# Weight quantisation chunks moved from the projection stage into the attention loop of an eight-core transformer layer

## What is computed

```python
xn = _layernorm(x)                                  # x: 16 x 2048 x 1024, f32
q, k, v = xn @ w_q, xn @ w_k, xn @ w_v              # 1024 -> 128, one head
s = (softmax(q @ k.T / sqrt(128)) @ v * mask) @ w_o
scale = max(abs(kernel)) / 7                        # kernel: 1024 x 1024
w = clip(round(kernel / scale), -8, 7) * scale
g = silu(xn @ w + bias + (xn @ a) @ b)
return x + s * g
```

## Time and profile before

| what | us |
|---|---|
| median of the runs (1221.0 and 1221.43) | 1221.22 |
| the profiled execution's own time | 1224.67 |
| its span on the slowest core, core 4 | 1222.8 |
| spans of the eight cores | 1209.9 to 1222.8 |
| mean granted TensorE clock of the cores | 0.909 to 0.917 |

### The profile page before, as it was taken

The page is one execution under the profiler, slowest core; times in us unless marked ns, Lnnn a source line. Parts: engine busy times, 40 slices in busy tenths (PEclk is TensorE's granted clock), DMA queues, the critical chain, the costliest instruction groups (busy, mean ns, idle before and its releaser), DMA issues.

```text
span 1222.8 us, 12399 instructions; the slowest of 8 cores (1209.9 to 1222.8 us)
## 1 busy us (share of the span) xinstructions
PE 923.5 (76%) x4453; PEld 499.5 (41%) x4453; DVE 428.5 (35%) x632; ACT 347.6 (28%) x662; POOL 21.8 (2%) x30
## 2 busy tenths in 40 slices
PE   0745363788885988888892789788885888989795
PEld 0422131466662334343431454366664333334332
DVE  2646755333323122221304665423332123132303
ACT  1322331554541211102011343445452110112110
POOL 4010000000000000000000000000000000000000
PEclk9987786899996999999997799999997989899998
DMA  5440301000001105150314320000001104123032
GB/s 142 148 139 23 121 24 45 18 1 1 1 1 69 69 1 172 35 172 35 103 35 172 127 115 1 0 2 1 1 1 69 35 35 155 53 71 136 3 135 104
DMA packets 25310, 78.54 MB, mean 64 GB/s; under 512 B 3601, under 2 KB 6673, under 8 KB 25250
## 3 DMA queue, kind: packets, MB, share of 16 engines
q1 hardware_dynamic: 18338, 52.57, 13.5%
q10 hardware_dynamic: 4608, 16.78, 3.4%
q0 software_dynamic: 2304, 8.39, 2.1%
HBM read 60.95 MB, written 16.78 MB: 64 GB/s over the span
## 4 chain that ended last, share of the span: by engine, by line
PE 59%; DVE 14%; ACT 12%; DMA 8%; issue 6%; POOL 0%; DVEq 0%; ACTq 0%; SPq 0%; POOLq 0%
PE PA L162 47%; PE PS L162 6%; PE PF L162 6%; ACT xfh L199 3%; DMA y<-xq 3%; DVE xfl L417 3%; ACT A_sb L208 3%; ACT ATf L199 3%; DVE g_sb L194 2%; DMA wstpair<-kern 2%; DVE xq L189 2%; DVE ssum L234 1%; DMA wstpair<-x 1%; DVE nm L234 1%; DMA wstpair<-wq 1%
## 5 line engine op out<-in xcount | busy, mean ns | idle before, releaser
L162 PE MATMUL PA<-xfh,q_sb 128*128 128x512 bf16 x512 | 132.0, 404 | 7.3 <-ACT g_sb L208 3.8
L162 PE MATMUL PA<-ATf,Vt 128*128 128x256 f32 x512 | 114.3, 381 | 18.2 <-ACT ATf L199 18.2
L208 ACT ACTIVATE g_sb<-PA,invsc 128x512 f32<-128x512 f32 x64 | 43.7, 687 | 279.8 <-PE PA L162 241.6
L162 PE MATMUL PA<-xfl,q_sb 128*128 128x512 bf16 x512 | 122.7, 383 | 0.0
L417 DVE TENSOR_TENSOR xfl<-PF,xfh 128x1024 bf16<-128x1024 f32 x32 | 39.2, 1225 | 229.9 <-ACT xfh L199 229.9
L162 PEld LDWEIGHTS PA<-ATf,Vt 128*128 128x128 f32 x512 | 96.0, 190 | 37.5 <-issue 25.1
L208 ACT ACTIVATE A_sb<-PS,nmax 128x512 f32<-128x512 f32 x128 | 86.3, 686 | 78.6 <-DVE nmax L234 78.6
L234 DVE TENSOR_REDUCE nm<-PS 128x1 f32<-128x512 f32 x128 | 81.8, 687 | 35.1 <-PE PS L162 34.8
L162 PE MATMUL PS<-identf,xn_tm 128*128 128x128 f32 x256 | 39.4, 314 | 68.3 <-DVE xn_tm L183 56.0
L162 PE MATMUL PF<-identf,xn_tm 128*128 128x128 f32 x256 | 45.7, 337 | 51.6 <-DVE xfl L417 41.2
L162 PEld LDWEIGHTS PA<-xfh,q_sb 128*128 128x128 bf16 x512 | 48.4, 102 | 81.4 <-issue 40.3
(11 more groups left out here) (131 smaller groups left out, 1149.8 us busy)
## 6 DMA issues: line engine op xcount, KB each, us to landing
wstpair<-x SPq DMA_DIRECT2D x64, 512.0 KB, 4.7
xq<-x SPq DMA_DIRECT2D x32, 512.0 KB, 4.9
y<-xq ACTq DMA_DIRECT2D x32, 512.0 KB, 5.6
wstpair<-kern POOLq DMA_DIRECT2D x16, 512.0 KB, 4.1
wstpair<-wq SPq DMA_DIRECT2D x1, 512.0 KB, 10.8
wstpair<-wk SPq DMA_DIRECT2D x1, 512.0 KB, 10.7
wstpair<-wv SPq DMA_DIRECT2D x1, 512.0 KB, 4.0
wstpair<-wo SPq DMA_DIRECT2D x1, 512.0 KB, 3.7
```

What stands on the lines that cost most here:

```text
L162: e.matmul(o, l, r, start=st, stop=sp, is_transpose=t))
L208: e.activation(o, i, f, bias=b, scale=s, accum_out=a)),
```

## The change

Of the eight chunks only three stay in the projection stage, one in each of the iterations 2, 3 and 4. The other five are emitted in the attention loop of the first sequence, each at the end of a block: chunk 3 after block 2, 4 after 5, 5 after 8, 6 after 11, 7 after 14. The release of the staging buffers to stage 3 moves behind chunk 7. The number of instructions is the same.

```diff
                 elif it == 2:
                     pa_free[0] = quant_stage1(pa_free[0])
-                    quant_chunks([0, 1, 2])
+                    quant_chunks([0])
                 elif it == 3:
-                    quant_chunks([3, 4, 5])
+                    quant_chunks([1])
                 elif it == 4:
-                    quant_chunks([6, 7])
-                    xrel_free[0] = kst_free[0]
-                    xrel_free[1] = kst_free[1]
+                    quant_chunks([2])
...
             if qb >= 1:
                 a_transposes(qb - 1)
+            if quant and qb in (2, 5, 8, 11, 14):
+                quant_chunks([3 + (2, 5, 8, 11, 14).index(qb)])
+                if qb == 14:
+                    xrel_free[0] = kst_free[0]
+                    xrel_free[1] = kst_free[1]
```

## The result

The changed kernel takes 1.0038 times the time of the kernel before (95% interval 1.0023 to 1.0052): 1227.81 us median over 15 runs beside 1222.9 us over 14 runs of before, some 4.6 us slower by the ratio. Some executions run longer, with less clock granted to a die; ratios and their intervals leave these out, medians do not. The forecast was +4.2 us. The profiled execution took 1227.44 us, with a span of 1225.5 on core 4.

The account below looks back on a forecast made before the run. The kernel was taken as bound by matmuls, with stretches where TensorE waits for VectorE and ScalarE. Attention's cost of 37.8 us less the projection stage's gain of 33.6 gave +4.2: 1225.4 us, range 1215 to 1232, forecast chance 62%.

Parts of the forecast that it names:

- Iteration 2: Projection stage: without chunks 1 and 2 the last tile's row sums end 11.7 us earlier, then limited by a late load.
- V of that iteration at half clock: Projection stage, V's matmuls in iteration 2: no gain counted from the clock; worth up to 2.8 us if that was wrong.
- Iteration 3: Projection stage: one chunk of three stays, fully hidden; Vf to Vf falls to the second sequence's 22.6 us, gaining 14.8 us.
- Iteration 4: Projection stage: one chunk of two stays in front of the first block's maxima; gain one chunk, 7.1 us.
- The waits in attention: First sequence's attention: each chunk delays what stands behind it, 5.3 us after even blocks, 6.9 after odd ones.
- The clock: Attention: matmuls run at half clock behind each chunk's gap, costing 2.1 us after even blocks, 0.9 after odd ones.
- the first scores behind an even chunk: Attention, after even blocks: the first matmuls of the scores run at half clock, 0.3 us of the 2.1 us clock cost.
- Rival A: Attention's idle engine time swallows the five chunks, so only the 33.6 us gain is left: 1187.6 us; chance 3%.
- Rival B: The clock holds in attention, which pays only waits of 29.7 us: net -3.9, 1217.3 us; chance 23%.
- Rival C: Half clock lasts beyond the first matmul group after each attention gap: 49.9 us cost, net +16.3, 1237.5 us; chance 11%.
- the sign I gave for it: Slow clock behind each attention gap: from about 5 us per gap the slower rival, Rival C, was to hold.

Follow-up runs that it names:

- x5_late_row: The changed kernel with the small bias-row load on SyncE's queue issued behind the last tile's four loads; 1.0053 of the kernel before.
- x3_filled: The changed kernel with matmuls whose results nobody reads put into TensorE's five attention gaps; 1217.33 us median, 0.9948 of the kernel before.
- x4_woven5: The changed kernel with its five attention chunks cut into pieces, each placed where its engine waits anyway; 1185.3 us median, 0.9682 of the kernel before.
- x10_both_again: Repeat of x7_woven6_late: six chunks in pieces in attention and the bias-row load issued later, against the changed kernel; 0.9714 of the kernel before.
- x7_woven6_late: x6_woven6 and x5_late_row together: six chunks in pieces in attention and the bias-row load issued later; no ratio, only one run could be compared.
- x6_woven6: As x4_woven5 with chunk 2 moved too: six chunks in pieces in attention, two left in the projection stage; 0.9676 of the kernel before.

## Why the prediction was right

The direction, the size and the parts came out. How close the net came (4.6 or 4.7 us, forecast 4.2) is partly luck: it is a small difference of two sums, each of which was off by up to 1.3 us, and nothing made these errors cancel. Point by point:

- Iteration 2: 11.7 us forecast, 11.6 measured (29.0 to 17.4 us from invsc to the end of the sums, median of the cores), and 12.7 in the four other profiles with this stage. The step that made it was to ask what is late next: without the two chunks' 14.3 us the load costs 2 to 3 of them. x5_late_row showed the load as the cause, and the small load in front of it as what held it back.
- V of that iteration at half clock: I counted no gain, and its first eight matmuls still took 3.57 us behind a gap of 7.96 us.
- Iteration 3: 14.8 us forecast, 14.6 measured as a median of the cores (37.2 to 22.6 us from Vf to Vf). The second sequence was the measure for how the first would run without chunks, and the one chunk left is hidden: Ql is written at 160.42, before the copy of K's remainder (164.50), and VectorE waits 3.80 us for V's matmuls before Vf, as in the second sequence.
- Iteration 4: 7.1 forecast, 16.3 - 9.1 = 7.2 measured.
- The waits in attention, read from x3_filled, where the clock stays up: each hTl is late by what the chunks before it cost. The even blocks cost 5.1 to 5.5 us each (5.3 forecast), the odd ones 6.7 and 7.1 (6.9 forecast).
- The clock, read as the changed kernel less x3_filled: 2.3 to 2.5 us behind each even chunk (2.1 forecast) and 0.7 to 0.8 behind each odd one (0.9 forecast), 8.8 in all instead of 8.1. The term that was sized low is the first scores behind an even chunk. I counted 0.3 us for them, but five of the twelve are spaced at half clock: the first starts 1.68 us later than in x3_filled (216.28 and 214.60), and nmax behind them 2.78 us later (221.39 and 218.61).
- hTl to hTl over block 5's chunk is 26.1 us where it was 18.5, so 7.7 where 6.9 + 0.9 was forecast.
- Rival A failed on the place: the idle time was there, and x4_woven5 put the chunks into it. Rival B had the waits right to 0.1 us in sum (29.8 measured, 29.7 forecast) and lacked the clock.
- Rival C's cost did not come, but the sign I gave for it, about 5 us of slow clock per gap, was no good sign. On the eight cores TensorE stayed slow for 4.3 to 5.7 us behind the gaps, and longest behind even chunks, where sixteen transposes and twelve scores would have to be slow before C's price is reached. At 252.75 the av_pair behind an odd chunk is back at full speed (16 in 3.62 us, half of 7.14 for 32).

## What to carry to other kernels

In an engine's list, what moved work cost here was not its duration but the delay of the instruction behind it, less that instruction's old idle time. Cut the work where the dependence chain crosses engines, and put each piece in front of an instruction with enough idle time before it; read the result by whether that idle time has stayed above zero. And price a wait on TensorE twice: once for the wait, once for the matmuls at half clock behind it (here 8.8 us on 29.8).

## What the runs showed of the hardware

Filling a gap with useless matmuls paid: 124 of them took 8.8 us off attention.

In six of the profiles (x5_late_row to x10_both_again, on two chips) some cores had long phases at a granted clock of 0.81, between the two levels, and always in pairs (0 and 1, 2 and 3, 4 and 5, 6 and 7). Attention of core 3 in x7_woven6_late, the phase alone, and its TensorE timeline within:

```profile
168.00:337.00 169.00, 149.78 (x705) 104.68 (x703) 76.78 (x144) 93.47 (x213) 2.11 (x4) 0.86 0.06 19
212.40:337.00 124.60, 114.47 (x517) 81.85 (x515) 54.47 (x98) 65.44 (x145) 1.58 (x3) 0.81 0.07 22
```

```profile
226.18 0.44 PE L162 MATMUL PS<-Kh,Qh 128*128 128x512 bf16 x1
...
227.77 8.66 PE L162 MATMUL PA<-ATf,Vt 128*128 128x256 f32 x32 [0.63 <-ACT ATf L199]
```

The av_pair takes 8.66 us instead of 7.14 with no gap before it longer than before, and stretch 2 of that core is 167.8 us where its other cores have down to 153.8. In x6_woven6 the same befell cores 4 and 5 in the second sequence's last stage, and core 4 ends at 1190.2 us where cores 0 to 3 end at 1170.9 to 1180.4. What brings it on was not tried. It lengthens the slowest core in some executions and may be why the last comparisons are unclear; that is not shown.
